# Selective state-space block with an MLP: convolution products of two taps by 64 channels on the column halves of TensorE, factors of decay, carry and halo as register and constants

## The chip, the cores and the metric

One core of a Trainium2 chip. The metric is device microseconds of one execution; the time before is the median of 3 runs, 2728.4 us (2726.94 to 2728.78).

## The reference

The input x is [4, 2048, 256] in float32. Two residual blocks follow each other.

```python
x = x + mamba(layernorm(x))
x = x + mlp(layernorm(x))

def mamba(x):                      # D_INNER 512, D_STATE 16, D_CONV 4
    xp, res = split(x @ W_in.T)    # 2 x 512
    xc = silu(conv(xp) + conv_b)   # causal, depthwise, 4 taps
    B, C, dt = split(xc @ W_x.T)   # 16, 16, 1
    dt = softplus(dt @ W_dt.T + b_dt)
    # for each t: h = exp(A * dt) * h + dt * B * xc ; y = h . C + D * xc
    return silu(y + res) @ W_out.T

def mlp(x):                        # ternary weights with scales, hidden 1024
    h = silu(x @ w1.T * s1) * (x @ w2.T * s2)
    h = gelu(h @ h1.T * t1)
    h = gelu(h @ h2.T * t2)
    return h @ w3.T * s3
```

## The kernel before, in words

The kernel has two stages. The first works in chunks of T = 256 tokens, 32 chunks, eight for each of the four sequences (PER_SEQ), with the channels on the partitions: 512 channels are ET = 4 groups e of P = 128. The second stage does the last layers of the MLP in blocks of 512 tokens; the change does not touch it.

In the first stage a body for chunk c runs the scan of chunk c over its 16 states n and, between the steps of the scan, the pieces of work of other chunks: `norm` for chunk c + 2, `front` (convolution, Silu, ssm, dt) for c + 1, `post` (gate, output projection) for c - 1, and `mlp` for c - 1 and the three before it. Ahead of the bodies the pipeline fills with norm(0), front(0) and norm(1). Where each piece stands is written by hand: `PE_AT` for TensorE has 32 places for each body (place 2n + q stands behind the transposes of state n, token half q), `ACT_AT` for ScalarE 32, `DVE_AT` for VectorE 48, `POOL_AT` for GpSimd and `SP_AT` for the DMA queue 16. The `mlp` pieces count on through several bodies (place 64 + k is place k of the third body). Every engine works off its queue in order, and engines wait for each other by semaphores.

One state n takes these steps. GpSimd makes the product ub = u * B (L872). ScalarE makes the decay exp(dt * neg_a[n]) in two halves of 128x510 into one of three PSUM banks (L1207), so it can be at most three halves ahead of the scan. VectorE scans each half (L1408), h = decay * h + ub. TensorE transposes h (L1756, two groups of four). VectorE adds C * h to y for both token halves (L1421); the transposes of the next state into the same bank wait for that. ScalarE copies the last column of h into `carry` for the next chunk (L1179), times a `keep` that is 0 at the end of a sequence and 1 elsewhere, read from a column in SBUF.

The convolution: TensorE projects the input onto two banks, xp0 and xp1 (L1638), each with two groups e of 128 channels by 256 tokens. ScalarE copies the last three tokens to the front as a halo (L1054) and each bank into `xp` (L989, in `take`), at places 2 and 5. For each e and each of the four taps TensorE multiplies a diagonal 128x128 matrix with `xp`, moved by the tap (L1656):

```python
for tap in range(first_tap, first_tap + TAPS // 2):
    last = nc.tensor.matmul(into[:, i * T:(i + 1) * T], conv_diag[:, e, tap], xp[:, e, tap:tap + T],
                            start=(tap == 0), stop=(tap == TAPS - 1))
```

ScalarE applies Silu (L1137) at place 10, in a block in which it loads the table of Silu (L1165), does the convolution's four groups and the gate's (L1143), and loads the table of exp back (L1173). It also makes `act_high` (L1126), a rounded copy of the gated MLP values, at places 2, 2, 3 and 6; GpSimd subtracts it to get `act_low` (L899) behind the states 1, 2, 3 and 4; the hidden layer on TensorE (L1744) starts at place 7 and waits for the last of the four `act_low`. A product in float32 is two TensorE instructions; those of the MLP layers, rounded to high and low parts, are one each.

## Time and profile before

| | |
|---|---|
| median of the runs | 2728.4 us |
| the runs | 2726.94, 2728.40, 2728.78 us |
| span of the profiled execution | 2725.9 us |
| own time of the profiled execution | not given beside its span; the median of the runs is 2.5 us above the span |
| one scan body in the middle of the first stage | 63.52 us |
| TensorE busy in the span | 2555.0 us |
| VectorE busy | 2349.3 us |
| ScalarE busy | 2217.3 us |
| GpSimd busy | 2168.3 us |
| mean granted clock of TensorE | 0.982 |

Times in the profile are microseconds from the start of the span, unless marked ns. A row of a timeline gives the start, the duration, the engine (PE is TensorE, DVE VectorE, ACT ScalarE, POOL GpSimd), the line of the kernel, the operation, what it writes and reads, and how many like it stand together; in brackets is the idle time of the engine before it and who ended it. Instructions on one engine overlap by a part of their durations, so a group of four is shorter than four times one. L989 is the line of `take`, which copies a bank.

### The profile page before, as it was taken

Reading aid. Unit: us, or ns where it says so; the run is one execution under the profiler, and the core shown is the slowest. Engines: PE = TensorE matmul, PEld = TensorE weight load, DVE = VectorE, ACT = ScalarE, POOL = GpSimd, SP = SyncE. Lnnn points to the kernel's source line nnn. Section 1 sums busy time; section 2 is a strip of 40 time slices with the busy share of each in tenths; the row PEclk is TensorE's granted clock in tenths of the full one; section 3 lists DMA queues with packets and bytes.
Section 4 is the critical chain, followed back from the end, with each engine's and each line's share of the span. In section 5 each row is a group of like instructions: output and inputs, shape, how many; then the busy total and the mean of one; then the engine's idle time right before and its main releaser. Section 6 shows DMA issues by size and latency. Waiting matters only on the chain. (4 is left out here: it accounts for less than half of the span.)

```text
span 2725.9 us, 52681 instructions
## 1 busy us (share of the span) xinstructions
PE 2555.0 (94%) x18562; PEld 2339.7 (86%) x18562; DVE 2349.3 (86%) x2767; ACT 2217.3 (81%) x4560; POOL 2168.3 (80%) x1696
## 2 busy tenths in 40 slices
PE   6679999999999999999999999999987999999999
PEld 5558888888888888888888888888877899999999
DVE  4999999999999999999999999999994277777676
ACT  7898888888888888888888888888877677777774
POOL 3788888888888888888888888888884586676763
PEclk8889999999999999999999999999989999999999
DMA  6112211211121112121112112111132222222220
GB/s 235 39 49 65 70 59 60 71 59 59 60 67 60 63 60 71 63 72 66 60 59 71 59 59 63 63 59 63 60 139 66 78 78 94 93 94 94 93 94 33
DMA packets 130187, 199.01 MB, mean 73 GB/s; under 512 B 16384, under 2 KB 93312, under 8 KB 129920
## 3 DMA queue, kind: packets, MB, share of 16 engines
q1 hardware_dynamic: 129920, 195.57, 22.0%
q8 instruction: 153, 2.51, 0.4%
q14 instruction: 114, 0.93, 0.1%
HBM read 144.68 MB, written 50.86 MB: 72 GB/s over the span
## 5 line engine op out<-in xcount | busy, mean ns | idle before, releaser
L1408 DVE TENSOR_TENSOR_SCAN h<-banks,ub 128x512 f32<-128x512 f32 x1024 | 1195.6, 1205 | 40.9 <-ACT banks L1207 34.0
L872 POOL TENSOR_TENSOR ub<-u,b_row 128x1020 f32<-128x1020 f32 x512 | 1216.5, 2376 | 0.3 <-issue 0.2
L1421 DVE SCALAR_TENSOR_TENSOR acc<-banks,c_tok,acc 128x512 f32<-128x512 f32 x1024 | 717.8, 735 | 77.5 <-PE banks L1756 77.2
L1207 ACT ACTIVATE banks<-dt,neg_a 128x510 f32<-128x510 f32 x1024 | 698.8, 687 | 67.1 <-DVE h L1408 66.0
L1756 PE MATMUL banks<-ident,h 128*128 128x128 f32 x4096 | 598.9, 278 | 100.6 <-DVE acc L1421 64.2
L1756 PEld LDWEIGHTS banks<-ident,h 128*128 128x128 f32 x4096 | 479.6, 143 | 189.5 <-DVE h L1408 108.9
L1744 PE MATMUL banks<-act_high,h_rounded 128*128 128x256 f32 x2048 | 515.7, 291 | 8.3 <-POOL act_low L899 6.7
L1744 PE MATMUL banks<-act_low,h_rounded 128*128 128x256 f32 x2048 | 495.6, 281 | 0.0
L1744 PEld LDWEIGHTS banks<-act_high,h_rounded 128*128 128x128 f32 x2048 | 388.7, 190 | 15.0 <-issue 14.4
L1744 PEld LDWEIGHTS banks<-act_low,h_rounded 128*128 128x128 f32 x2048 | 389.2, 190 | 0.1
L871 POOL TENSOR_TENSOR ub<-b_u,enter 128x4 f32<-128x4 f32 x512 | 106.2, 207 | 262.5 <-DVE h L1408 253.5
L1730 PE MATMUL banks<-xT_high,w_rounded 128*128 128x256 f32 x1024 | 266.2, 296 | 7.8 <-ACT silu L1152 3.7
L1656 PE MATMUL banks<-xp,conv_diag 128*128 128x256 f32 x1024 | 252.2, 379 | 2.5 <-ACT xp L989 2.5
L1730 PE MATMUL banks<-xT_low,w_rounded 128*128 128x256 f32 x1024 | 251.6, 280 | 0.0
L1730 PEld LDWEIGHTS banks<-xT_high,w_rounded 128*128 128x128 f32 x1024 | 193.2, 189 | 10.8 <-ACT silu L1152 5.5
L1656 PEld LDWEIGHTS banks<-xp,conv_diag 128*128 128x128 f32 x1024 | 179.4, 190 | 20.4 <-issue 2.9
L1730 PEld LDWEIGHTS banks<-xT_low,w_rounded 128*128 128x128 f32 x1024 | 193.7, 189 | 0.0
L1494 DVE TENSOR_TENSOR act_low<-quad,act_high 128x512 fp32r<-128x512 f32 x128 | 164.7, 1323 | 21.1 <-ACT act_high L1295 21.1
L899 POOL TENSOR_TENSOR act_low<-silu,act_high 128x512 fp32r<-128x512 f32 x128 | 163.8, 1281 | 22.8 <-ACT act_high L1126 22.7
L1179 ACT ACTIVATE carry<-h,keep 128x4 f32<-128x4 f32 x510 | 153.0, 300 | 32.0 <-DVE h L1408 32.0
L938 POOL TENSOR_TENSOR T_low<-T_raw,T_high 128x1024 fp32r<-128x1024 f32 x46 | 135.9, 2956 | 36.2 <-ACT T_high L1250 34.8
L1638 PE MATMUL banks<-xnT,w_in_sb 128*128 128x256 f32 x512 | 128.6, 397 | 28.1 <-ACT xnT L989 28.1
(157 smaller groups left out, 5514.8 us busy)
## 6 DMA issues: line engine op xcount, KB each, us to landing
b_row<-b_scratch SPq DMA_DIRECT2D x128, 512.0 KB, 4.0
z_scratch<-z_out SPq DMA_DIRECT2D x128, 256.0 KB, 2.1
zl_raw<-z_scratch SPq DMA_DIRECT2D x32, 1024.0 KB, 7.1
x_sb<-in_x SPq DMA_DIRECT2D x32, 256.0 KB, 4.3
x_res<-in_x SPq DMA_DIRECT2D x32, 256.0 KB, 3.3
h_full<-in_h SPq DMA_DIRECT2D x2, 4096.0 KB, 18.1
x_scratch<-x_sb SPq DMA_DIRECT2D x32, 256.0 KB, 2.8
out_e<-x_scratch SPq DMA_DIRECT2D x16, 512.0 KB, 3.9
```

The costliest lines, as they stand in the source:

```text
L872: nc.gpsimd.tensor_tensor(ub[:, n % 2, :, 1:], u[:, :, 1:], b_row[:, n // QUARTER % 2, n % QUARTER:n % QUARTER + 1, 1:].to_broadcast([P, E ...
L899: nc.gpsimd.tensor_tensor(act1_low[c % 2][:, 2 * p:2 * p + 2], silu1[:, p], act1_high[c % 2][:, 2 * p:2 * p + 2].bitcast(F32), ALU.subtrac ...
L938: nc.gpsimd.tensor_tensor(low_of(name, blk), raw_of(name, blk), t_high[name][:].bitcast(F32), ALU.subtract).then_inc(low_t, 1)
L1179: nc.scalar.activation(carry[:, n, :], h[:, n % 2, :, T - 1], ACT.Copy, scale=keep[:, c + 1:c + 2]).then_inc(carry_ready, 1)
L1207: nc.scalar.activation(decay_half(k)[:, :, 1:], dt[:, par, 2 * i:2 * i + 2, 1:], ACT.Exp, scale=neg_a[:, n:n + 1]).then_inc(decay_ready, 1)
L1408: nc.vector.tensor_tensor_scan(h[:, n % 2, 2 * i:2 * i + 2].rearrange("p e t -> p (e t)"), banks[:, k % DECAYS, :], ub[:, n % 2, 2 * i:2 * ...
L1421: nc.vector.scalar_tensor_tensor(out=acc[:, par, q], in0=turned[q], scalar=c_tok[:, par, q, n:n + 1], in1=acc[:, par, q], op0=ALU.mult, op ...
L1494: nc.vector.tensor_tensor(low, rows, high.bitcast(F32), ALU.subtract).then_inc(split2, 1)
L1656: last = nc.tensor.matmul(into[:, i * T:(i + 1) * T], conv_diag[:, e, tap], xp[:, e, tap:tap + T], start=(tap == 0), stop=(tap == TAPS - 1))
L1730: last = nc.tensor.matmul(into[:, i * T:(i + 1) * T], weights[:, d, o * P:(o + 1) * P], rows[:, d], start=(d == 0 and rows is xT_high), st ...
L1744: last = nc.tensor.matmul(into[:, i * T:(i + 1) * T], rounded["h1"][:, k, o * P:(o + 1) * P], rows[c % 2][:, k], start=(k == 0 and rows is ...
L1756: last = nc.tensor.transpose(turned[q][:, e * P:(e + 1) * P], h[:, n % 2, e, q * P:(q + 1) * P], ident[:])
```

## The change

Convolution: a stationary matrix now holds two taps of 64 channels on its 128 rows and 64 output columns. For each e there are four products, (b, h) with b the pair of taps and h the half of the channels; h chooses the column half of the array and the half of the output partitions. So `xp` is stored twice: for each channel half h, the lower 64 partitions hold the channels and the upper 64 the same channels one token ahead. ScalarE fills it by four copies of 64 partitions for each bank (half by odd) in place of one of 128. The matrices are made from a folded identity. The convolution's pieces stand at places 1, 2, 4 and 5, before at 0 to 5.

Factors: `keep` is no longer a tensor; carry and halo take a constant 0.0 or 1.0 as scale. The decay's scale is read from a register of ScalarE; the 16 registers are loaded from `neg_a` once, before the first decay.

Around it: the conv weights come in another order in DRAM, `xp` is twice as large, and so is its memset; two memsets of `keep` go, and the waits on `setup` count 6 and 7 in place of 7 and 9.

```diff
@@ -91,13 +92,13 @@
-        conv_diag = sb("conv_diag", [P, ET, TAPS, P], where=a_only)
+        conv_diag = sb("conv_diag", [P, ET, 2, TAPS // 2, HP], where=a_only)
-        xp = sb("xp", [P, ET, HALO + T], where=a_only)
+        xp = sb("xp", [P, ET, 2, HALO + T], where=a_only)
@@ -112,13 +113,13 @@
-        conv_w_sb = sb("conv_w_sb", [P, ET, TAPS], where=a_only)
+        conv_w_sb = sb("conv_w_sb", [P, ET, 2, TAPS // 2], where=a_only)
+        folded = sb("folded", [P, HP], where=a_only)
-        keep = sb("keep", [P, CHUNKS + 1], where=a_only)
@@ -286,6 +288,10 @@
+        def keep(c):
+
+            return 0.0 if c % PER_SEQ == 0 and c < CHUNKS else 1.0
+
@@ -296,7 +302,7 @@
-            front={0: ('conv0.a',), 1: ('conv0.b',), 2: ('conv0.c', 'conv0.d'), 3: ('conv1.a', 'conv1.b'), 4: ('conv1.c',), 5: ('conv1.d',), 10: ('ssm.a',), 11: ('ssm.b',), 13: ('dtc',), 23: ('acc0.a', 'acc0.b', 'acc0.c'), 25: ('acc1.a', 'acc1.b', 'acc1.c')},
+            front={1: ('conv0.a',), 2: ('conv0.b',), 4: ('conv1.a',), 5: ('conv1.b',), 10: ('ssm.a',), 11: ('ssm.b',), 13: ('dtc',), 23: ('acc0.a', 'acc0.b', 'acc0.c'), 25: ('acc1.a', 'acc1.b', 'acc1.c')},

@@ -304,7 +310,7 @@
-        LAST_PIECE = {"uu": "b", "gg": "b", "h": "d", "xp": "b", "conv": "d", "ssm": "b", "acc": "c", "out": "d"}
+        LAST_PIECE = {"uu": "b", "gg": "b", "h": "d", "xp": "b", "conv": "b", "ssm": "b", "acc": "c", "out": "d"}
@@ -658,12 +664,12 @@
-            sp.dma_start(conv_w_sb[:], conv_w.rearrange("(e p) o k -> p e (o k)", p=P)).then_inc(weights_in, 16)
+            sp.dma_start(conv_w_sb[:], conv_w.rearrange("p (e h b) -> p e h b", e=ET, h=2)).then_inc(weights_in, 16)
-            sp.wait_ge(setup, 7)
+            sp.wait_ge(setup, 6)
@@ -801,15 +807,13 @@
-            nc.gpsimd.memset(keep[:], 1.0).then_inc(setup, 1)
-            pool.wait_ge(setup, 7)
+            pool.wait_ge(setup, 6)
-            nc.gpsimd.memset(keep[:, 0:CHUNKS:PER_SEQ], 0.0).then_inc(setup, 1)
-            pool.wait_ge(setup, 9)
+            pool.wait_ge(setup, 7)
@@ -1051,9 +1055,16 @@
             def project(c, j):
                 if j == 0:
                     wait_full(act, "xp0", c)
-                    nc.scalar.activation(xp[:, :, 0:HALO], xp[:, :, T:T + HALO], ACT.Copy, scale=keep[:, c:c + 1]).then_inc(halo_ready, 1)
+                    rows = xp[:].rearrange("p e h t -> p (e h) t")
+                    nc.scalar.activation(rows[:, :, 0:HALO], rows[:, :, T:T + HALO], ACT.Copy, scale=keep(c)).then_inc(halo_ready, 1)
                     act.wait_ge(halo_ready, c + 1)
-                take(f"xp{j}", c, xp[:, 2 * j:2 * j + 2, HALO:], bank(f"xp{j}", c).rearrange("p (e t) -> p e t", e=2))
+                wait_full(act, f"xp{j}", c)
+                rows = bank(f"xp{j}", c).rearrange("p (e t) -> p e t", e=2)
+                for half in range(2):
+                    for odd in range(2):
+                        at = HALO - odd
+                        last = nc.scalar.activation(xp[HP * odd:HP * (odd + 1), 2 * j:2 * j + 2, half, at:at + T], rows[HP * half:HP * (half + 1)], ACT.Copy)
+                last.then_inc(freed(f"xp{j}", c), 1)
 
             def front(c, n):
                 par = c % 2
@@ -1176,7 +1187,7 @@
-                nc.scalar.activation(carry[:, n, :], h[:, n % 2, :, T - 1], ACT.Copy, scale=keep[:, c + 1:c + 2]).then_inc(carry_ready, 1)
+                nc.scalar.activation(carry[:, n, :], h[:, n % 2, :, T - 1], ACT.Copy, scale=keep(c + 1)).then_inc(carry_ready, 1)
@@ -1191,10 +1202,14 @@
+            rate = [nc.scalar.alloc_register(f"rate{n}") for n in range(NS)]
+
+                    for n in range(NS):
+                        nc.scalar.reg_load(rate[n], neg_a[0:1, n:n + 1].bitcast(I32))
@@ -1204,7 +1219,7 @@
-                        nc.scalar.activation(decay_half(k)[:, :, 1:], dt[:, par, 2 * i:2 * i + 2, 1:], ACT.Exp, scale=neg_a[:, n:n + 1]).then_inc(decay_ready, 1)
+                        nc.scalar.activation(decay_half(k)[:, :, 1:], dt[:, par, 2 * i:2 * i + 2, 1:], ACT.Exp, scale=rate[n]).then_inc(decay_ready, 1)
@@ -1369,13 +1384,16 @@
-            dve.wait_ge(setup, 9)
+            dve.wait_ge(setup, 7)
+                nc.vector.tensor_tensor(folded[:], ident[:, 0:HP], ident[:, HP:P], ALU.add).then_inc(fold_done, 1)
+                dve.wait_ge(fold_done, 1)
-                    for k in range(TAPS):
-                        nc.vector.tensor_scalar(conv_diag[:, e, k], ident[:], conv_w_sb[:, e, k:k + 1], None, ALU.mult)
+                    for h in range(2):
+                        for b in range(TAPS // 2):
+                            nc.vector.tensor_scalar(conv_diag[:, e, h, b], folded[:], conv_w_sb[:, e, h, b:b + 1], None, ALU.mult)
@@ -1646,16 +1664,16 @@
                     job, part = (piece.split(".") + [""])[:2]
                     into = wait_bank(job, c) if part in ("", "a") else bank(job, c)
                     if job.startswith("conv"):
-                        j, quarter = int(job[-1]), "abcd".index(part)
-                        i, first_tap = quarter // 2, TAPS // 2 * (quarter % 2)
+                        j, i = int(job[-1]), "ab".index(part)
                         e = 2 * j + i
                         if c == 0 and e == 0 and part == "a":
                             pe.wait_ge(diag_ready, 1)
                         wait_taken(pe, f"xp{j}", c)
-                        for tap in range(first_tap, first_tap + TAPS // 2):
-                            last = nc.tensor.matmul(into[:, i * T:(i + 1) * T], conv_diag[:, e, tap], xp[:, e, tap:tap + T],
-                                                    start=(tap == 0), stop=(tap == TAPS - 1))
-                        if quarter == 3:
+                        for b in range(TAPS // 2):
+                            for h in range(2):
+                                last = nc.tensor.matmul(into[HP * h:HP * (h + 1), i * T:(i + 1) * T], conv_diag[:, e, h, b], xp[:, e, h, 2 * b:2 * b + T],
+                                                        start=(b == 0), stop=(b == TAPS // 2 - 1))
+                        if i == 1:
                             last.then_inc(job_full, 1)
                     elif job == "ssm":
                         if c == 0 and part == "a":
@@ -1892,8 +1910,12 @@
 
         return np.ascontiguousarray(v.reshape(-1, P).T)
 
+    def taps_by_halves(w):
+
+        return np.ascontiguousarray(w.reshape(-1, 2, HP, 2, 2).transpose(4, 2, 0, 1, 3).reshape(P, -1))
+
     arrays = {
-        "x": a["attn_x"], "w_in": turn(a["attn_W_in"]), "conv_w": a["attn_conv_w"], "conv_b": columns(a["attn_conv_b"]),
+        "x": a["attn_x"], "w_in": turn(a["attn_W_in"]), "conv_w": taps_by_halves(a["attn_conv_w"]), "conv_b": columns(a["attn_conv_b"]),
         "w_x": turn(a["attn_W_x"]), "w_dt": columns(a["attn_W_dt"]), "b_dt": columns(a["attn_b_dt"]),
         "a_log": a["attn_A_log"], "d_skip": columns(a["attn_D"]), "w_out": turn(a["attn_W_out"]),
         "w1": turn(a["ffn_w1_w"]), "s1": columns(a["ffn_w1_s"]), "w2": turn(a["ffn_w2_w"]), "s2": columns(a["ffn_w2_s"]),
```

## Rows read from the trace of the kernel before

**Rows 1.** The page: span, busy time of the engines, one of the costliest groups.
```profile
span 2725.9 us, 52681 instructions
...
PE 2555.0 (94%) x18562; PEld 2339.7 (86%) x18562; DVE 2349.3 (86%) x2767; ACT 2217.3 (81%) x4560; POOL 2168.3 (80%) x1696
...
L1656 PE MATMUL banks<-xp,conv_diag 128*128 128x256 f32 x1024 | 252.2, 379 | 2.5 <-ACT xp L989 2.5
```
**Rows 2.** View of one line, the scan: duration, first and last start.
```profile
L1408 DVE TENSOR_TENSOR_SCAN h<-banks,ub x1024: 1191/1208/1225, 40.4 to 2076.9; 128x512 f32<-128x512 f32 x171
```
**Rows 3.** Table by stretches, one scan body: busy time and instructions, clock, DMA.
```profile
core 0: us, PE busy (x) PEld busy (x) DVE busy (x) ACT busy (x) POOL busy (x), PEclk, DMA share, GB/s
994.50:1058.02 63.52, 61.28 (x437) 55.04 (x437) 60.35 (x73) 54.67 (x120) 55.26 (x49) 1.00 0.20 63
```
**Rows 4.** Timeline of VectorE in that body: start, duration; in brackets idle time before.
```profile
1002.52 1.38 DVE L1421 SCALAR_TENSOR_TENSOR acc<-banks,c_tok,acc 128x512 f32<-128x512 f32 x2
...
1012.99 1.22 DVE L1408 TENSOR_TENSOR_SCAN h<-banks,ub 128x512 f32<-128x512 f32 x1 [0.86 <-ACT banks L1207]
...
1017.67 1.38 DVE L1421 SCALAR_TENSOR_TENSOR acc<-banks,c_tok,acc 128x512 f32<-128x512 f32 x2
...
1025.94 0.75 DVE L1421 SCALAR_TENSOR_TENSOR acc<-banks,c_tok,acc 128x512 f32<-128x512 f32 x1 [0.46 <-PE banks L1756]
...
1037.32 0.75 DVE L1421 SCALAR_TENSOR_TENSOR acc<-banks,c_tok,acc 128x512 f32<-128x512 f32 x1 [1.22 <-PE banks L1756]
1038.71 0.75 DVE L1421 SCALAR_TENSOR_TENSOR acc<-banks,c_tok,acc 128x512 f32<-128x512 f32 x1 [0.64 <-PE banks L1756]
```
**Rows 5.** Timeline of TensorE in the same body.
```profile
1000.41 1.89 PE L1656 MATMUL banks<-xp,conv_diag 128*128 128x256 f32 x8
...
1008.21 0.35 PE L1744 MATMUL banks<-act_high,h_rounded 128*128 128x256 f32 x1
...
1017.44 0.60 PE L1756 MATMUL banks<-ident,h 128*128 128x128 f32 x4
...
1022.09 0.63 PE L1756 MATMUL banks<-ident,h 128*128 128x128 f32 x4 [0.27 <-DVE acc L1421]
```
**Rows 6.** Timeline of ScalarE in the same body, first 18 us.
```profile
994.10 0.31 ACT L1054 ACTIVATE xp<-xp,keep 128x12 f32<-128x12 f32 x1 [0.20 <-PE banks L1638]
994.43 0.60 ACT L989 ACTIVATE xp<-banks 128x512 f32<-128x512 f32 x1
995.75 0.69 ACT L1207 ACTIVATE banks<-dt,neg_a 128x510 f32<-128x510 f32 x1 [0.71 <-DVE h L1408]
...
1001.78 0.62 ACT L1126 ACTIVATE act_high<-silu 128x512 fp32r<-128x512 f32 x1
...
1006.24 0.30 ACT L1179 ACTIVATE carry<-h,keep 128x4 f32<-128x4 f32 x1 [0.49 <-DVE h L1408]
...
1007.14 1.28 ACT L1165 ACT_TABLE_LOAD   x1
...
1012.27 0.69 ACT L1207 ACTIVATE banks<-dt,neg_a 128x510 f32<-128x510 f32 x1
```
**Rows 7.** Timeline of ScalarE, groups of two and four alike.
```profile
1008.43 1.57 ACT L1137 ACTIVATE xc<-banks,conv_b_sb 128x256 f32<-128x256 f32 x4
...
1020.85 1.07 ACT L989 ACTIVATE gT<-banks 128x512 f32<-128x512 f32 x2
...
1022.68 1.94 ACT L1075 ACTIVATE sig<-banks,b_dt_sb,w_dt_sb 128x256 f32<-128x256 f32 x4
```
**Rows 8.** Timeline of GpSimd in the same body.
```profile
1003.08 1.29 POOL L899 TENSOR_TENSOR act_low<-silu,act_high 128x512 fp32r<-128x512 f32 x1
...
1006.77 1.29 POOL L899 TENSOR_TENSOR act_low<-silu,act_high 128x512 fp32r<-128x512 f32 x1
```
**Rows 9.** Timeline of ScalarE while the pipeline fills.
```profile
23.46 0.84 ACT L1137 ACTIVATE xc<-banks,conv_b_sb 128x256 f32<-128x256 f32 x2 [2.14 <-PE banks L1656]
...
37.22 1.90 ACT L1207 ACTIVATE banks<-dt,neg_a 128x510 f32<-128x510 f32 x3
```
**Rows 10.** View of one line, the load of the flag into a register.
```profile
L616 ACTq TENSOR_LOAD <-flag x1: 466/466/466, 2170.2 to 2170.2; - x1
```

More of the change, by code:

```diff
@@ L32 @@
 P = 128
+HP = P // 2
 EPS = 1e-5
@@ L43, in program @@
     DI = w_out.shape[0]
-    TAPS = conv_w.shape[-1]
+    TAPS = 4
     NS = a_log.shape[0]
@@ L236, in program @@
         diag_ready = sem("diag_ready")
+        fold_done = sem("fold_done")
         x_in = sem("x_in")
@@ L769, in both @@
                     if not (isinstance(first_value, int) and isinstance(second_value, int)):
-                        sp.wait_ge(setup, 7)
+                        sp.wait_ge(setup, 6)
                     after(sp, first, values[0])
@@ L984, in _ @@
             nc.scalar.preload_act_table_set("natural_log_exp_and_others")
-            act.wait_ge(setup, 9)
+            act.wait_ge(setup, 7)
             def take(name, c, dst, src):
@@ L1569, in stats_b @@
                     last.then_inc(bn_b_done, 1)
-                    dve.wait_ge(setup, 9)
+                    dve.wait_ge(setup, 7)
                     dve.wait_ge(bn_b_done, c + 1)
@@ L1614, in _ @@
         def _(pe):
-            pe.wait_ge(setup, 9)
+            pe.wait_ge(setup, 7)
             def select(row):
```

## The prediction, made before the changed kernel ran

> **What bounds the kernel now.** I read the page first: the span is 2725.9 us and TensorE is busy 94% of it, VectorE 86% [rows 1]. Those are averages over two stages, so next comes the table by stretches. The 32 scan bodies start at 40.4 us and the last scan starts at 2076.9 [rows 2]; one body in the middle lasts 63.52 us, with TensorE busy 61.28, VectorE 60.35, ScalarE 54.67 and GpSimd 55.26 [rows 3]. Everything the change touches is in these bodies and in the filling of the pipeline ahead of them; the stage behind them has none of it.
>
> Two engines are nearly full, so I read the timeline of VectorE to see what interrupts it. In that body it idles four times, 3.18 us together: 0.86 us before the scan at 1012.99, released by ScalarE's decay, and 0.46, 1.22 and 0.64 us before the y additions at 1025.94, 1037.32 and 1038.71, released by TensorE's transposes [rows 4]. So what sets the end is VectorE's work plus these waits. A change is worth what it does to them.
>
> The waits on TensorE first. TensorE started the transposes at 1022.09 after idling 0.27 us for VectorE's y addition [rows 5]. It had caught up, and what makes it late at 1025.94 and 1037.32 is work issued after 1022.09: hidden layer, output projection, first MLP layer. The convolution (997.8 to about 1006.9) is ahead of that point. TensorE time saved there ends in a longer idle time before 1022.09.
>
> The wait on ScalarE: it starts a table load at 1007.14, does the two Silu groups, loads the table back, and reaches the next decay at 1012.27 [rows 6]. VectorE uses up the decays made ahead and stands at 1012.99.
>
> **Prices.** A copy of 128x512 from a bank: two of them take 1.07 us and one 0.60 [rows 6, 7], so the next one starts 0.48 us after. A ScalarE operand that is a column in SBUF: four 128x256 activations with scale and bias from columns take 1.94 us, four with only the bias 1.57 [rows 7], the last of each included, thus 0.09 us for each column. A convolution product is two TensorE instructions: eight take 1.89 us [rows 5]; with 0.379 for one alone [rows 1] they start 0.216 us apart, and the 32 of a chunk cost 6.9 us.
>
> **The change, part by part.**
> *Taps in pairs.* Still 16 products of 256 columns for each chunk, 32 instructions, but with 64 output columns each. No row shows two products side by side, so the bounds are nothing saved (6.9 us) and half (3.45 us saved). I take half, since the two halves of the array share no output; it hardly matters. Its new places 4 and 5 stand behind the transposes of n = 2, and these wait for the first y addition of the pair at 1002.52, which ends at 1003.3 [rows 4]. From there, unpaired: four groups of transposes (0.60 us [rows 5], of which the last 0.16 overlap the successor as with the products, thus 0.44) and 16 instructions of 0.216 (3.46 us): with a hand-over 1008.6. The next work, gated as below, cannot start before 1008.9. So body time moves by 0 in both cases.
> The Trainium skill, TensorEngine Tiling (Array Packing), Key Properties, says that changing the tiling mode drains TensorE; no run here shows it. Worked out from the row, a drain would be about 0.38 - 0.22 = 0.16 us; eight switches make 1.3 us on TensorE, after which the paired convolution still ends earlier than today, and the sum stays as it is.
>
> *Copies of xp.* Each of xp0 and xp1 becomes four copies of 64x512 in place of one of 128x512. No row has 64 partitions read from a bank; the bounds are the full 0.48 us each and half of it. ScalarE's rows scale with elements for each partition, so I take 0.48: 6 more copies, +2.88 us for each chunk.
>
> *Columns turned into constants and a register.* In each body 32 decays, 16 carries and one halo lose 0.09 us each: -4.4 us. For the register no row exists; bounds are 0.09 saved and nothing saved; I take 0.09: a value that comes with the instruction has no column to fetch. In total ScalarE gets 1.5 us shorter for each body. But order decides: the additions come at 994 and 1000 us, before the two points that matter, and most of the savings come after.
>
> *First point: the third act_high* (old start 1001.78 [rows 6]). From xp0 full (994.10) to there: +2.88 us; minus 4 decays, 2 carries and the halo, 7 x 0.09 = 0.63; minus the idle time of 0.71 before 995.75, 0.83 with the overlap that a wait forfeits. It comes 1.42 us later and ends at 1003.82 instead of 1002.40. GpSimd's act_low, which subtracts it, started at 1003.08 [rows 8] and now, a hand-over behind 1003.82, 0.75 us later. Behind it in GpSimd's queue are the ub products and the last act_low (1006.77, 1.29 us). That one gates TensorE's h layer, which started at 1008.21, right behind it [rows 5, 8]; it moves by 0.75. From there TensorE runs without a gap to the transposes of 1017.44, which end at 1018.04 [rows 5]; VectorE's second addition of the pair at 1017.67 starts at 1018.31 [rows 4], so 0.27 us are cover. VectorE is late by 0.75 - 0.27 = 0.48 us. The y addition which releases TensorE at 1022.09 moves by the same, and so does all the rest of the body.
> (The ub product in between reaches the scan at 1007.37 some 0.25 us late; that is swallowed by the wait at 1012.99.)
>
> *Second point: the table load.* To the carry at 1006.24: +2.88, minus 7 decays, 3 carries and the halo (0.99), minus idle time, 0.83 and, with the overlap, 0.57: 0.49 late. The carry and decay in front of the block and the decay behind it give back 0.27. The wait of 0.86 becomes 1.08: +0.22, less than 0.48. VectorE is held at the addition of 1018.31 until 0.48 past its old time whichever of the two came before, so the larger one counts.
>
> *Filling the pipeline.* Paired convolution of chunk 0 saves about 0.6 us (ScalarE idled 2.14 us for its second half, at 23.46 [rows 9]; it now ends earlier, though the copies ahead of it take longer). The 16 rates are now loaded into registers ahead of the first decay, at 37.22 [rows 9]. One load took 466 ns [rows 10]; bounds are 16 in series, 7.5 us, and wholly overlapped, about 0.5. I take series. The first scan stood 2.5 us behind its first decay (which ends at 37.22 + 0.69 = 37.91; the scan starts at 40.4 [rows 2, 9]), so it comes 7.5 - 0.6 - 2.5 = 4.4 us later; with small recoveries +3.9 for the whole fill. GpSimd's larger memset of xp (about +0.8 us) hides behind the first load of x. conv_diag is made of narrower tiles and waits for a DMA anyway.
>
> **Sum.** The full pattern stands in 28 bodies (c = 3 to 30): 28 x 0.48 = 13.4; bodies 1 and 2: 0.2; fill: 3.9. Together +17.5 us on the profiled span: 2743.4. The median of the runs, 2728.4, lies 2.5 us over that span, so 2746.
>
> **Rivals.**
> 1. ScalarE gets ahead: faster. If the additions before 1006.24 cost no more than what is idle or saved there (1.40 + 0.99 us against 2.88), the block starts on time and the wait of 0.86 shrinks by 0.27: 28 x 0.27 = 7.6 us, and 0.6 at the start, with overlapped register loads: 2720. It decides at 0.40 us for a copy in place of 0.48, for the table load (2.39 / 6) and for act_high too (0.67 + 0.27 us of cover there, so 2.40 / 6). For it: the margin is small. Against: no copy of 512 elements is that cheap here. Chance 0.20.
> 2. The register saves nothing. Then act_high is 1.78 late and VectorE 0.84; the table load is 0.49 + 0.63 late, less 0.09 for the carry, so the wait grows by 1.03. 28 x 1.03 + 4.1 = 33: 2761. Chance 0.10.
> 3. The effects cancel: GpSimd or TensorE has a tenth or two more cover, register loads overlap: 2726 to 2732. Chance 0.14.
> 4. TensorE is the bound, as its 61.28 of 63.52 us suggests. Then 3.45 us for each body would remove all 2.32 us of waits on it: 28 x 2.32 = 65: 2663. Against: the idle time at 1022.09 and the place of the convolution. Chance 0.04. The Trainium skill, TensorEngine Tiling (Array Packing), Theoretical Speedup, gives up to 2x for a dimension of 64; this would be that rule carried through to the time.
> 5. The pairs do not run side by side, the change not doing what it says: body as forecast, start 1.1 us worse, 2747. It is inside the forecast.
>
> **How the numbers follow.** Forecast and 5 together 0.52. A measurement can tell about 0.2%, 5.5 us, from no change. Slower: 0.50 of the forecast and rival 2, 0.60. Same: rival 3, 0.04 of rival 1, 0.02 of the forecast: 0.20. Faster: 0.16 of rival 1 and rival 4: 0.20. The range goes from rival 1 to rival 2: 2719 to 2761. Within the forecast alone, copies of 0.45 to 0.50 us and loads overlapped or not give 2735 to 2750.
>
> **What would show it.** Right: bodies of 64.0 us; GpSimd's third act_low waiting for ScalarE; eight xp copies 0.48 us apart; decays near 0.60 us; a burst of 16 loads before the first decay; TensorE's busy time down by 3 us for each body and its idle time before the h layer up. Wrong: decays still at 0.69 (rival 2), copies under 0.40 (rival 1), VectorE's waits at 1025.94 and 1037.32 gone (rival 4). I would be wrong above all if a tenth or two of cover in the chain ScalarE, GpSimd, TensorE, VectorE was misread, since 28 bodies multiply it.

## The result

| | before | after |
|---|---|---|
| median of the runs, same chip | 2727.7 us | 2783.6 us (2783.0 to 2784.1) |
| ratio of after to before | | 1.0208, 95% interval 1.0194 to 1.0221 |
| span of the profiled execution | 2725.9 us | 2781.9 us |
| first scan starts at | 40.4 us | 44.3 us |
| bodies 3 to 30, mean | 63.52 us | 65.41 us |
| last body's start to the end of the span | 715.0 us | 709.5 us |

The changed kernel is slower, as forecast (2746), but the loss is three times the forecast one, and the time lies above the range (2719 to 2761). The span grew by 56.0 us: 3.9 in the fill, 4.8 in the bodies 0 to 2, 28 x 1.89 = 52.9 in the bodies 3 to 30, and 5.5 came back behind them.

The page of the changed kernel, the rows that answer to [rows 1] first:

```profile
span 2781.9 us, 52887 instructions
...
PE 2500.0 (90%) x18562; PEld 2226.2 (80%) x18562; DVE 2355.8 (85%) x2768; ACT 2197.0 (79%) x4752; POOL 2166.4 (78%) x1694
...
L1222 ACT ACTIVATE banks<-dt 128x510 f32<-128x510 f32 x1024 | 605.0, 595 | 84.5 <-DVE h L1426 78.9
...
L1066 ACT ACTIVATE xp<-banks 64x512 f32<-64x512 f32 x256 | 151.6, 592 | 4.1
...
L1674 PE MATMUL banks<-xp,conv_diag 128*64 128x256 f32 x1024 | 144.1, 404 | 6.8 <-ACT xp L1066 6.8
```

The parts did what they are meant to do. The convolution's products took 144.1 us of TensorE in place of 252.2, and ScalarE's busy time is 20 us lower though it has 192 instructions more. Neither number tells that the kernel is slower. The table by stretches shows where to look; its columns are those of [rows 3], and the rows are body 14, body 15 and bodies 3 to 30 together:

```profile
961.24:1027.78 66.54, 60.59 (x438) 52.55 (x437) 60.77 (x74) 53.85 (x126) 55.37 (x49) 0.97 0.19 61
1027.78:1093.16 65.38, 59.44 (x438) 51.41 (x437) 60.75 (x74) 53.99 (x126) 55.32 (x49) 1.00 0.19 62
240.92:2072.39 1831.47, 1664.45 (x12195) 1439.86 (x12193) 1700.31 (x2017) 1510.43 (x3487) 1548.76 (x1343) 0.99 0.19 61
```

Body 15 is the one that [rows 3 to 8] show of before; its start is 33.28 us later here. All engines together are idle more; one is late and the rest wait. ScalarE's timeline of that body, the counterpart of [rows 6]:

```profile
1027.39 0.23 ACT L1059 ACTIVATE xp<-xp 128x24 f32<-128x24 f32 x1 [0.71 <-PE banks L1656]
1027.65 2.40 ACT L1066 ACTIVATE xp<-banks 64x512 f32<-64x512 f32 x4
1029.95 0.58 ACT L1222 ACTIVATE banks<-dt 128x510 f32<-128x510 f32 x1
1030.56 0.63 ACT L1137 ACTIVATE act_high<-silu 128x512 fp32r<-128x512 f32 x1
...
1033.88 0.58 ACT L1222 ACTIVATE banks<-dt 128x510 f32<-128x510 f32 x1
1034.48 2.40 ACT L1066 ACTIVATE xp<-banks 64x512 f32<-64x512 f32 x4
1036.91 0.21 ACT L1190 ACTIVATE carry<-h 128x4 f32<-128x4 f32 x1
1037.02 0.58 ACT L1222 ACTIVATE banks<-dt 128x510 f32<-128x510 f32 x1
1037.54 0.61 ACT L1137 ACTIVATE act_high<-silu 128x512 fp32r<-128x512 f32 x1
...
1041.76 1.28 ACT L1176 ACT_TABLE_LOAD   x1
```

Four copies take 2.40 us, 0.60 each: they don't overlap at all, while two copies of 128x512 took 1.07 us in [rows 7]. The act_high at 1037.54 stood at 1001.78 in [rows 6]: 9.76 us behind the body's first scan in place of 7.28, so 2.48 us late. GpSimd and TensorE follow:

```profile
1038.23 1.27 POOL L903 TENSOR_TENSOR act_low<-silu,act_high 128x512 fp32r<-128x512 f32 x1 [1.83 <-ACT act_high L1137]
...
1041.91 1.27 POOL L903 TENSOR_TENSOR act_low<-silu,act_high 128x512 fp32r<-128x512 f32 x1
```

```profile
1043.33 0.36 PE L1762 MATMUL banks<-act_high,h_rounded 128*128 128x256 f32 x1 [1.24 <-POOL act_low L903]
```

The hidden layer started at 1008.21 in [rows 5] and starts at 1043.33 - 33.28 = 1010.05 here, 1.84 late. VectorE feels both delays, that of the decays and that of the hidden layer:

```profile
1047.52 1.22 DVE L1426 TENSOR_TENSOR_SCAN h<-banks,ub 128x512 f32<-128x512 f32 x1 [0.57 <-ACT banks L1222]
...
1053.38 0.75 DVE L1439 SCALAR_TENSOR_TENSOR acc<-banks,c_tok,acc 128x512 f32<-128x512 f32 x1 [0.45 <-PE banks L1774]
```

The first row is the scan behind ScalarE's table block, at 1012.99 in [rows 4]: 1047.52 - 33.28 = 1014.24, 1.25 late. The second is the addition that the forecast names, at 1018.31 before: 1020.10, 1.79 late, and it waits here for the transposes behind the hidden layer, as it didn't before. The body is 1.86 us longer.

### The profile page after: what moved, and what is told of

Its sections match the earlier page's. It is cut to its first block and busy times, and to the rows that moved or that the text cites. A ratio compares the mean times of both kernels' runs of the same rounds, so it can differ in the third digit from the quotient of the medians.

```text
span 2781.9 us, 52887 instructions
## 1 busy us (share of the span) xinstructions
PE 2500.0 (90%) x18562; PEld 2226.2 (80%) x18562; DVE 2355.8 (85%) x2768; ACT 2197.0 (79%) x4752; POOL 2166.4 (78%) x1694
## 5 line engine op out<-in xcount | busy, mean ns | idle before, releaser
L1774 PE MATMUL banks<-ident,h 128*128 128x128 f32 x4096 | 606.6, 281 | 178.9 <-DVE acc L1439 136.9
L1774 PEld LDWEIGHTS banks<-ident,h 128*128 128x128 f32 x4096 | 470.4, 143 | 303.4 <-DVE h L1426 223.3
L1222 ACT ACTIVATE banks<-dt 128x510 f32<-128x510 f32 x1024 | 605.0, 595 | 84.5 <-DVE h L1426 78.9
L1762 PE MATMUL banks<-act_high,h_rounded 128*128 128x256 f32 x2048 | 524.6, 294 | 39.4 <-POOL act_low L903 39.1
L1762 PE MATMUL banks<-act_low,h_rounded 128*128 128x256 f32 x2048 | 504.3, 285 | 0.0
L1762 PEld LDWEIGHTS banks<-act_high,h_rounded 128*128 128x128 f32 x2048 | 394.6, 193 | 46.3 <-issue 45.7
L1066 ACT ACTIVATE xp<-banks 64x512 f32<-64x512 f32 x256 | 151.6, 592 | 4.1
L1674 PE MATMUL banks<-xp,conv_diag 128*64 128x256 f32 x1024 | 144.1, 404 | 6.8 <-ACT xp L1066 6.8
L1411 DVE SCALAR_TENSOR_TENSOR silu<-banks,scales,silu 128x256 f32<-128x256 f32 x256 | 108.7, 483 | 47.3 <-ACT silu L1163 46.7
```

The lines of the kernel that those rows point to most:

```text
L1066: last = nc.scalar.activation(xp[HP * odd:HP * (odd + 1), 2 * j:2 * j + 2, half, at:at + T], rows[HP * half:HP * (half + 1)], ACT.Copy)
L1222: nc.scalar.activation(decay_half(k)[:, :, 1:], dt[:, par, 2 * i:2 * i + 2, 1:], ACT.Exp, scale=rate[n]).then_inc(decay_ready, 1)
L1674: last = nc.tensor.matmul(into[HP * h:HP * (h + 1), i * T:(i + 1) * T], conv_diag[:, e, h, b], xp[:, e, h, 2 * b:2 * b + T], start=(b == 0 ...
L1762: last = nc.tensor.matmul(into[:, i * T:(i + 1) * T], rounded["h1"][:, k, o * P:(o + 1) * P], rows[c % 2][:, k], start=(k == 0 and rows is ...
L1774: last = nc.tensor.transpose(turned[q][:, e * P:(e + 1) * P], h[:, n % 2, e, q * P:(q + 1) * P], ident[:])
```

## The experiments

Twelve kernels were run, on three chips; each ratio is against runs of before on the same chip, and the 2727.7 us of the first row are those of the section above. For each kernel the table gives the start of the late act_high behind the first scan of body 15 (1001.78 - 994.50 = 7.28 in before [rows 3, 6]), and the mean of the bodies 3 to 30 (the stretch from the first scan of body 3 to that of body 31, divided by 28).

| kernel | late act_high | mean body | median of the runs | ratio to before (95%) |
|---|---|---|---|---|
| before | 7.28 | 63.52 | 2727.7 | 1 |
| factors only | 6.84 | 63.32 | 2716.5 | 0.9958 (0.9944 to 0.9971) |
| factors, loads spread | 6.83 | 63.33 | 2714.8 | 0.9953 (0.994 to 0.9967) |
| factors, three copies more, first bank | 7.75 | 63.37 | 2721.0 | 0.9974 (0.9964 to 0.9985) |
| factors, three copies more, second bank | 8.48 | 63.91 | 2737.7 | 1.0037 (1.0024 to 1.0049) |
| factors, six copies more | 9.38 | 64.78 | 2769.5 | 1.0154 (1.0137 to 1.0171) |
| split copies | 8.31 | 63.94 | 2741.7 | 1.005 (1.0032 to 1.0069) |
| after | 9.76 | 65.41 | 2783.6 | 1.0208 (1.0194 to 1.0221) |
| after, products twice | 9.75 | 65.17 | 2778.9 | 1.0194 (1.0179 to 1.021) |
| after, other order of copies | 9.75 | 65.41 | 2784.0 | 1.0217 (1.0201 to 1.0233) |
| after, late act_high moved ahead | 3.31 | 64.70 | 2765.1 | 1.0138 (1.0122 to 1.0153) |
| after, one copy per bank | 6.82 | 63.36 | 2713.5 | 0.995 (0.9935 to 0.9965) |
| taps only | 10.40 | 67.01 | 2837.6 | 1.0401 (1.0385 to 1.0417) |
| taps only, products twice | 10.40 | 66.14 | 2813.0 | 1.031 (1.0293 to 1.0327) |

The late act_high is the one at place 6, the only one behind the second bank's copies. The prediction calls it the third, after the act_low that waits for it; of ScalarE's own four it is the last. Where a body has longer decays (columns), the same start goes with a somewhat longer body.

### The two halves of the change alone

Factors only is the kernel before with the register and the constants:

```diff
-ACT.Exp, scale=neg_a[:, n:n + 1])
+ACT.Exp, scale=rate[n])
-scale=keep[:, c + 1:c + 2]
+scale=keep(c + 1)
```

> The kernel before with the factors alone: constants for carry and halo, a register for decay; convolution and copies as before. Theory C (the six added copies of xp on ScalarE are the loss): bodies of 63.25 us, 0.27 under before, since the wait on the decay behind the table load shrinks from 0.86 to 0.58; the 16 loads take 4.9 us and put the first scan 2.4 us later; 2720 to 2726 us. Rival F (the register is the loss, for instance because a register operand holds up ScalarE's queue): slower than before, 2735 us or more. Rival T (TensorE is the loss, through its mode changes and a clock that falls when it idles): 2728 us, as before.

Measured 2716.5 us, below what was expected. The bodies of 63.32 are close to the expected 63.25; the bodies 0 to 2 take 5.0 us less together, which wasn't expected. It beats the kernel before by 0.42%.

Taps only is the changed kernel with `keep` and `neg_a` read from columns again.

> The changed kernel with the columns back: paired taps and eight copies, but keep and neg_a as operands in SBUF. Theory C: ScalarE is later still by some 0.6 us at the table load, bodies of about 66.0 us, first scan back by 4 us; 2790 to 2800 us. Rival F: 2728 us, as before. Rival T: 2780 us, as the changed kernel, since TensorE's work is the same.

Measured 2837.6, far above. Of the bodies 3 to 30 half last 66.2 us or less, near the expected 66.0, but 14 of 28 last 67.4 to 68.9 (the clock, below), and the bodies 0 to 2 take 203.8 us together in place of 191.9. The two halves don't add: -11 and +110 give +56. The factors save 0.20 us a body alone (63.52 to 63.32) and 1.60 behind the taps (67.01 to 65.41), 0.97 of it with a steady clock (66.14 to 65.17, the kernels with the products twice). Alone, most of what they save on ScalarE falls into time that it would have idled.

### The price of a copy

Split copies keeps the convolution of before and splits its copy:

```diff
-take(f"xp{j}", c, xp[:, 2 * j:2 * j + 2, HALO:], bank(f"xp{j}", c).rearrange("p (e t) -> p e t", e=2))
+for half in range(2):
+    part = slice(P // 2 * half, P // 2 * (half + 1))
+    for e in range(1 + j):
+        of = slice(e, e + 1) if j else slice(0, 2)
+        last = nc.scalar.activation(xp[part, 2 * j + of.start:2 * j + of.stop, HALO:], rows[part, of], ACT.Copy)
```

> The kernel before, each bank of xp copied in parts: the first bank as two copies of 64x512, lower rows then upper rows, the second as four of 64x256, two on the lower rows and two on the upper. It measures what keeps copies of 64 rows from overlapping. Theory R (fewer than 128 rows never overlap): 0.60 us from start to start for 64x512, 0.38 to 0.40 for every 64x256. Rival S (only a change of rows breaks the overlap): 0.60 for 64x512, but 0.27 between the two 64x256 on the same rows and 0.39 where the rows change. Rival O (the overlap is there and something else made the copies slow): 0.48 and 0.27. Time 2728 to 2735 us, as the 0.83 us of idle time in front of the decay takes most of it.

Measured: the two copies of 64x512 (other rows) start 0.603 us apart, no overlap. Of the four copies of 64x256 those on the same rows start 0.28 us apart with a duration of 0.38; where the rows change, 0.377. So it isn't the number of partitions but their change that takes the overlap away. The time, 2741.7, is above what was expected, because the late act_high comes 1.03 us later (8.31 against 7.28).

In after, the source's rows change at every second copy and the destination's at each. The next kernel swaps the loops, so that at two of three places only the source's rows change:

```diff
-for half in range(2):
-    for odd in range(2):
+for odd in range(2):
+    for half in range(2):
```

> The changed kernel with the eight copies in another order: for each bank first both halves' unshifted copies, then both shifted ones, so that other pairs of neighbours share their output rows. Theory S (any change of rows, of input or of output, takes the overlap of neighbouring instructions away): the copies start 0.60 us apart in every place, and the time stays at 2780 to 2786. Rival (only a change of the output's rows does): every second distance falls to 0.48 to 0.50, the body loses about 0.3 to 0.5 us, and the time is 2766 to 2774.

Measured 2784.0, and the four copies take the same time:

```profile
1027.83 2.41 ACT L1066 ACTIVATE xp<-banks 64x512 f32<-64x512 f32 x4
```

Either change is enough. The Trainium skill, VectorE: DVE Perf Modes, section Two Vector instructions with no wait between them, gives a rule of this kind for VectorE: an instruction whose input or output starts in another group of partitions than the last one in that memory waits until the earlier ones have finished. These runs show ScalarE doing the same, at 0.60 us in place of the 0.48 of copies on equal rows.

### Are the copies all of it?

One copy per bank keeps pairs, column halves and registers, and leaves out the copies that fill the second half and the shifted rows (its output isn't the reference's):

```diff
-for half in range(2):
-    for odd in range(2):
-        at = HALO - odd
-        last = nc.scalar.activation(xp[HP * odd:HP * (odd + 1), 2 * j:2 * j + 2, half, at:at + T], rows[HP * half:HP * (half + 1)], ACT.Copy)
+last = nc.scalar.activation(xp[:, 2 * j:2 * j + 2, 0, HALO:HALO + T], rows, ACT.Copy)
```

> The changed kernel with the pairs, the column halves and the registers kept, but with one copy over all 128 partitions for each bank (two a chunk, as in the kernel before) in place of eight over 64 partitions; the operands of the second half and of the shifted taps hold stale rows, so the output is not the reference's. Theory C (only the six added copies cost): bodies fall from 65.4 to about 63.3 us and the time to 2710 to 2722, beside the 2716 of the kernel with the registers alone. Rival T (the pairs themselves cost, by TensorE's mode changes or by the lower clock): bodies stay at 63.8 or more, the time over 2728.

Measured 2713.5, bodies 63.36: the six copies are the whole loss (a small part of it by way of the clock, which takes the shorter convolution too; see below). And the cheaper convolution is worth nothing: factors only has 63.32 with all full products. Both rows are bodies 3 to 30, this kernel first, then factors only:

```profile
226.33:2000.35 1774.02, 1656.09 (x12194) 1431.49 (x12193) 1690.89 (x2018) 1415.69 (x3319) 1549.25 (x1343) 1.00 0.19 63
```

```profile
228.99:2001.93 1772.94, 1711.99 (x12194) 1538.03 (x12193) 1691.62 (x2017) 1415.20 (x3319) 1549.55 (x1343) 1.00 0.20 64
```

TensorE is busy 55.9 us less in the first, and the stretch is 1.1 us longer.

Three kernels go the other way: factors only, with copies added that nobody reads, three behind each bank, or behind one of them:

```diff
+last = nc.scalar.activation(xp[:, 2 * j:2 * j + 2, HALO:], rows, ACT.Copy)
+for k in range((3, 3)[j]):          # (3, 0) and (0, 3) in the other two
+    half = (k + 1) // 2
+    to = (3 * j + k + 1) % 2
+    last = nc.scalar.activation(spare[HP * to:HP * (to + 1), (3 * j + k + 1) // 2 % 3], rows[HP * half:HP * (half + 1), :, :T - 12], ACT.Copy)
```

> The reverse of the kernel with one copy per bank: convolution by full products and the factors in registers, and six copies of 64 rows (488 columns) a chunk added, three behind each xp copy and ahead of the signal that frees the bank, into a buffer that nobody reads. Theory C (the added time on ScalarE alone makes the body longer): bodies 65.0 to 65.3 us and 2765 to 2778 us, against 63.32 and 2716 without them. Rival (column halves, their mode changes or the thinner TensorE load have a part in it): bodies 64.6 or less, under 2760.

> The same with only the three copies behind the first xp bank. The forecast's chain (late third activation, late low half on GpSimd, late second layer) runs through the second bank only, since the first bank's copies have idle time of ScalarE between them and the third activation. If that chain is all, bodies stay at 63.3 to 63.6 us, 2716 to 2726. Rival D (the decays behind the copies come late themselves): 64.0 or more, over 2735.

> The same with only the three copies behind the second xp bank. If the forecast's chain carries the loss, this kernel has nearly all of it: bodies 64.5 to 65.3 us, 2750 to 2775. Rival D (both banks delay decays alike): about half, 64.0 to 64.4.

Measured: six give 64.78 us a body, a little under what was expected, three at the first bank 63.37, as expected, three at the second 63.91, under both ranges given for it (64.5 to 65.3, and 64.0 to 64.4). The first bank alone costs 0.05, the second alone 0.59, both 1.46. They don't add, and the column of the late act_high says why. With the first bank's copies it starts at 7.75, 0.91 later, and the body doesn't change. At 8.48 the body is 0.59 longer, at 9.38 it is 1.46. Past about 7.9 each microsecond is paid in full: 63.91 - 8.48, 64.78 - 9.38 and, for after with a steady clock, 65.17 - 9.75 are 55.43, 55.40 and 55.42. The first bank's copies use up the slack; behind them the second's make the act_high 1.63 us later (7.75 to 9.38) and the body 1.41 us longer (63.37 to 64.78).

ScalarE with three copies at the second bank, then with six:

```profile
1006.50 0.58 ACT L1221 ACTIVATE banks<-dt 128x510 f32<-128x510 f32 x1
1007.01 0.58 ACT L1061 ACTIVATE xp<-banks 128x512 f32<-128x512 f32 x1
1007.49 1.73 ACT L1065 ACTIVATE spare<-banks 64x488 f32<-64x488 f32 x3
1009.12 0.20 ACT L1189 ACTIVATE carry<-h 128x4 f32<-128x4 f32 x1
```

```profile
1023.22 0.58 ACT L1221 ACTIVATE banks<-dt 128x510 f32<-128x510 f32 x1
1023.83 0.60 ACT L1061 ACTIVATE xp<-banks 128x512 f32<-128x512 f32 x1
1024.32 1.73 ACT L1065 ACTIVATE spare<-banks 64x488 f32<-64x488 f32 x3
```

The copy of 128 rows starts 0.51 us behind the decay in the first and 0.61 in the second. The decay doesn't read a bank; the last instruction that did was in the second kernel a copy from the rows 64 to 127. So what counts seems to be the last access to the same memory, not the neighbour. These two places agree with the rule cited above; no kernel was made for it.

### The chain through GpSimd

Three of the four act_high stand ahead of the second bank's copies, the late one behind them. One number in `ACT_AT` moves it ahead too:

```diff
-high=(66, 66, 67, 70)
+high=(66, 66, 67, 67)
```

> The changed kernel with the third act_high moved ahead of the second bank's copies (place 3 in place of 6). Theory C with its chain (copies, act_high, GpSimd's act_low, h layer on TensorE, y addition on VectorE): GpSimd no longer waits 1.8 us for ScalarE, the h layer starts about 1.5 us earlier; what is left is ScalarE's lateness at the table load, so bodies go from 65.4 to about 64.7 us; 2760 to 2772 us. Rival T: no change, 2783 us. Rival D (only the late decays hold VectorE, the chain through GpSimd is not felt): no change, 2781 to 2785 us.

Measured 2765.1 and 64.70, as expected. The copies still stand in ScalarE's queue, now only the decays behind them are late, which is the forecast's second point:

```profile
1028.30 2.34 DVE L1426 TENSOR_TENSOR_SCAN h<-banks,ub 128x512 f32<-128x512 f32 x2 [0.72 <-ACT banks L1222]
...
1037.57 1.22 DVE L1426 TENSOR_TENSOR_SCAN h<-banks,ub 128x512 f32<-128x512 f32 x1 [0.96 <-ACT banks L1222]
```

So there are two chains close to each other; taking one away gives back 0.7 of 1.9 us. The scan at 1037.57 stands 19.74 us behind the body's first scan, as in after (1047.52 - 1027.78), in place of 18.49: the late decays alone account for 1.25 us in both kernels, and the chain through GpSimd for what after loses beyond that.

### The granted clock

Of the bodies 3 to 30 of after, five (3, 8, 14, 20 and 25) are 66.5 to 66.9 us long, where the others are 65.4 at most, and have TensorE's clock at 1.2 GHz for 3.4 us; before has none such in that stretch. Stretches around one, in after; the clock is the column behind the busy times:

```profile
575.00:584.00 9.00, 5.59 (x42) 3.14 (x38) 7.84 (x10) 8.86 (x20) 7.18 (x6) 1.00 0.19 58
584.00:588.00 4.00, 3.91 (x20) 3.94 (x21) 3.62 (x4) 3.97 (x7) 4.00 (x5) 0.58 0.01 4
```

Ahead of it TensorE was busy only 5.59 of 9.00 us: short convolution, and a wait for the late act_low. Then the hidden layer, on the path that sets the body, runs at half rate. All 27 bodies from 3 to 29 have the same idle time in that place, and only five the low clock; what picks them isn't shown. Where the low clock falls decides what it costs: the kernel with the late act_high moved ahead has it in four bodies (15 to 18) for 3.4 us too, some 6 us earlier in the body and ahead of the hidden layer, and they are no longer than its others (64.84 and 64.70 us). Two kernels make TensorE busier without changing the results: each product is issued twice into the same bank, in after and in taps only.

```diff
-for b in range(TAPS // 2):
+for again_b in range(TAPS):
+    b = again_b % (TAPS // 2)
```

> The changed kernel with each convolution product issued twice into the same bank (same data, same result), so TensorE's convolution work, about 144 us over the run, is doubled. Theory C (the three us/2 of each body come from ScalarE's longer copies, through the late third activation, and TensorE only waits): TensorE has idle time where the products stand, so the time stays at 2776 to 2786 us. Rival G (the halves of the granted clock, 3.4 us each in some bodies, cost a visible part): a busier TensorE loses these dips and the time falls to 2770 to 2777. Rival P (TensorE is the bound after all): some 90 to 140 us more, 2870 or over.

> The kernel with the taps alone (column operands kept, 2837.6 us), its products issued twice. If the halves of the granted clock made the difference between its undisturbed bodies (66.22 us) and the mean (67.01), they vanish with the busier TensorE, the bodies come to 66.2 and the time to 2810 to 2820. Rival (the long bodies have another cause, the clock only follows): 2830 or more.

Measured: 2778.9 in place of 2783.6, and 2813.0 in place of 2837.6, faster with more work. The second is in the range expected of the clock. The first is small: it lies in the range of the theory that the time stays, and the intervals of the two ratios overlap; what speaks for it are the bodies, of which none is over 65.4 us. The clock stays at full rate over the whole stretch; taps only twice, then taps only:

```profile
245.46:2097.38 1851.92, 1755.34 (x13091) 1505.73 (x13089) 1704.14 (x2018) 1625.44 (x3487) 1549.86 (x1343) 1.00 0.19 61
```

```profile
985.32:1051.55 66.23, 59.58 (x437) 51.54 (x437) 60.88 (x74) 58.24 (x126) 55.45 (x49) 1.00 0.20 61
1051.55:1118.95 67.40, 60.92 (x437) 52.84 (x437) 61.12 (x73) 58.15 (x126) 55.47 (x49) 0.97 0.19 60
246.12:2122.30 1876.18, 1691.72 (x12194) 1466.63 (x12193) 1707.78 (x2018) 1626.72 (x3487) 1550.67 (x1343) 0.98 0.19 60
```

The clock was 0.87 us of taps only's body and 0.24 of after's: 28 x 0.24 = 6.7 us in the profiled executions, 4.7 between the medians.

### The register loads

```diff
 if n == ACT_AT["ssm"]:
+    load_rates(c, 7, 9)
 if n == ACT_AT["z"]:
+    load_rates(c, 9, 12)
 if n == ACT_AT["a_dt"]:
+    load_rates(c, 12, 16)
 for j in range(2):
+    if c == 0 and j == 1:
+        act.wait_ge(a_ready, 2)
+        load_rates(c, 0, 7)
```

> The kernel before with the factors in registers alone, and its sixteen register loads no longer in a block ahead of the first decay but spread over ScalarE's queue during the fill. If the loads cost the 1.8 us by which the first scan was late (42.17 against 40.37 us), the first scan comes back to 40.4 to 40.9 us and the time to 2714 to 2715.5 (from 2716.5). Rival: each load waits for its own DMA or for a cold fetch wherever it stands, and the first scan stays at 42.0 or later, the time at 2716 to 2718.

The line of the loads in this kernel (duration min, median, max; first and last start), then ScalarE's first decays in factors only and in this kernel:

```profile
L1043 ACTq TENSOR_LOAD <-neg_a x16: 273/280/483, 19.7 to 33.8; - x16
```

```profile
41.47 1.63 ACT L1212 ACTIVATE banks<-dt 128x510 f32<-128x510 f32 x3 [4.70 <-issue]
```

```profile
36.93 1.62 ACT L1219 ACTIVATE banks<-dt 128x510 f32<-128x510 f32 x3
```

The loads are hidden in ScalarE's idle time, the first scan starts at 40.3 in place of 42.2 us, and body 3 starts 2.3 us earlier. Behind the last body's start it takes 715.1 us, though, against 712.8 in factors only, and the median is only 1.7 us lower; the intervals of the two ratios overlap, so a gain of this kernel over factors only isn't shown. Its 2714.8 us are the lowest median of the kernels that compute what the reference does.

## Why the forecast was right in direction and wrong in size

**Taps in pairs.** Right. The pairs run side by side: in body 15 the products of both halves start 0.007 us apart and the next pair 0.27 and then 0.216 us later. Its place on the queue has idle time behind it, and the saving is worth nothing (one copy per bank against factors only). The drain was weighed at 0.16 us a switch; each switch is about 0.09 us longer than before (transposes to product 0.20 in place of 0.11 us, back 0.31 in place of 0.22), and that is hidden too. What the forecast didn't have is that the emptier TensorE drops to the lower clock in some bodies.

**Copies of xp.** This is the step that failed. It took 0.48 us for each of six added copies, +2.88 us a chunk, from a row of two copies on the same rows. They cost 0.60, and the two old ones became dearer too: 8 x 0.60 - 2 x 0.48 = 3.84. The bounds, 0.48 and half of it, had no side above: a loss of overlap wasn't thought of, though the duration of one copy (0.60) stood in the same row.

**Factors.** The register saves its column, as forecast: the decay takes 595 ns in place of 687, the carry 208 in place of 300. Ahead of the late act_high that saves 0.64 us behind the taps (10.40 in taps only, 9.76 in after), 0.63 forecast. In factors only it is 0.44 (7.28 to 6.84), since there the idle time of 0.71 before a decay takes up a part.

**First point, the late act_high.** The sum was 2.88 - 0.63 - 0.83 = 1.42 us late. Measured: 3.84 - 0.64 - 0.72 = 2.48, where 0.72 is what the idle time took up of the copies: in taps only the act_high comes 10.40 - 7.28 = 3.12 us later and not 3.84. Of the 1.06 us of miss 0.96 are the price of the copies and 0.11 the idle time. Then the forecast took 0.67 us of cover on GpSimd and 0.27 on TensorE off, 0.94 together; 2.48 us late made an undisturbed body 65.17 - 63.52 = 1.65 us longer, so the cover is 0.83. The chain ScalarE, GpSimd, TensorE, VectorE is the right one: the kernels with added copies lie on one line with it.

**Second point, the table load.** It starts at 1041.76 - 33.28 = 1008.48, 1.34 late in place of 0.49, by the same price of the copies. It is the smaller one as forecast, but close behind: VectorE is 1.25 us late by it and 1.79 at the addition that the first point holds, and with the first chain out of the way the waits on late decays set the body at 64.70.

**Fill.** +3.9 forecast, 3.9 measured, by a sum whose parts are off, so that the match is in part luck: behind the first a load takes some 0.30 us from start to start and not 0.466, so from the first start to the last of the sixteen it is 5.1 us, and the idle time before the first decay is 4.70 us, where 7.5 were taken.

```profile
L1212 ACTq TENSOR_LOAD <-neg_a x16: 273/280/476, 38.1 to 43.2; - x16
```

**Sum.** Forecast 28 x 0.48 = 13.4 us for the bodies 3 to 30, measured 52.9. Of the 39.5 between them 28 x 1.06 = 29.7 is lateness (copies 26.9, idle time 3.1, columns -0.3), 28 x 0.11 = 3.1 cover and 6.7 clock. The bodies 0 to 2 lose 4.8 us where 0.2 stood (196.7 in place of 191.9): the copies cost 10.2 there (186.5 with one copy per bank) and the factors alone give 5.0 back. The stretch behind the last body's start gives 5.5 back, which was not tried by itself. Kernels with equal work differ in that last stretch by 2.3 us (712.8 and 715.1, above), so part of the 5.5 may be chance.

**Rivals.** 1, 2 and 3 fell with the price of the copy and the shorter decays. 4, TensorE as the bound, is refuted from both sides: 55.9 us less work of TensorE gains nothing, and about 90 us more busy time in after costs nothing. 5 did not happen.

## What to carry to other kernels

A distance between equal instructions holds only for equal ones: when one instruction over all partitions becomes several over parts, take the whole duration of each. Follow the one piece of work that a later engine waits for, and add up what is put ahead of it; its slack is used up once, and from there every microsecond counts in each body. Before a product is made cheaper, see whether the engine idles behind it: here that saving had no value, and the copies that it needed cost about 70 us, 2.6% (2783.6 against 2713.5), while the factors in a register and constants alone gain 0.4%.

## What the runs showed of the hardware

- ScalarE: copies of 64x512 start 0.60 us apart when the start row of source or destination changes, of 128x512 0.48, of 64x256 0.28 on the same rows and 0.377 on others.
- ScalarE: a scale from a register saves as much as a constant does: the decay goes from 687 to 595 ns, the carry from 300 to 208, 92 ns each.
- A load into a register holds up ScalarE's queue: 476 ns the first, 280 the next, some 0.30 us from start to start.
- More products made the kernel faster: the granted clock, at 1.2 GHz for 3.4 or 6.8 us in 5 of 28 bodies of after and 14 of 28 of taps only, behind a wait of TensorE for the late act_low, stayed at 2.4 GHz, and taps only fell from 2837.6 to 2813.0 us.
